# Attention with its inputs prepared one slot ahead, fewer transfers for K and Q, and weight quarters issued by SyncE

## The reference

```
x   = x + tanh(g_xattn) * xattn(layernorm(x), ctx)     # x, ctx: (8, 256, 512) float32
x   = x + tanh(g_ffn)   * moe(layernorm(x))

xattn:  q = Wq x + bq;  k = Wk c + bk;  v = Wv c + bv   # 256 channels, 16 heads of 16
        p = softmax(q k^T / 4) over 512 positions;  out = Wo (p v) + bo
moe:    logits = tokens @ gate_w.T;  top 2 of 12 experts, weights normalized
        out  += (silu(t w1^T) * (t w3^T)) w2^T * weight  # 2048 tokens of 512, hidden 320
```

## Time and profile before

| | us |
|---|---|
| runs | 804.32, 808.91, 809.18 |
| median | 808.91 |
| profiled execution | 802.83 |
| its span | 801.1 |

### The profile page before, as it was taken

One profiled execution on the slowest core, in us unless ns is written; L12 is line 12 of the kernel. 1 busy time (PEld: TensorE's weight loads), 2 busy tenths in 40 slices (PEclk: granted clock), 3 DMA queues, 4 the chain that ended last, 5 costly groups with the idle time before them and its releaser, 6 DMA issues.

```text
span 801.1 us, 14200 instructions
## 1 busy us (share of the span) xinstructions
PE 621.2 (78%) x4169; PEld 270.8 (34%) x4170; DVE 420.0 (52%) x769; ACT 332.0 (41%) x394; POOL 243.0 (30%) x186
## 2 busy tenths in 40 slices
PE   3418849889698897988976523179999999999993
PEld 1101202213122131322311101156666666666661
DVE  4787546667466574657646652944333333333330
ACT  5216637567565666665684200002222222222221
POOL 5203105133141332314202111324444333544322
PEclk9959969999999999999997755569999999999997
DMA  5686886967949688695894747527587776764533
GB/s 159 172 221 179 209 248 172 217 205 194 274 134 249 184 179 256 151 275 165 181 283 150 209 152 262 211 79 208 121 234 201 225 205 185 196 114 83 91 40 41
DMA packets 75374, 146.54 MB, mean 183 GB/s; under 512 B 10757, under 2 KB 36870, under 8 KB 73798
## 3 DMA queue, kind: packets, MB, share of 16 engines
q1 hardware_dynamic: 43664, 68.18, 31.4%
q10 hardware_dynamic: 22038, 55.35, 22.7%
q0 software_dynamic: 9632, 22.55, 14.9%
HBM read 87.85 MB, written 53.74 MB: 177 GB/s over the span
## 4 chain that ended last, share of the span: by engine, by line
PE 43%; DMA 19%; issue 16%; DVE 8%; POOL 5%; SPq 5%; ACT 1%; POOLq 0%; DVEq 0%; ACTq 0%
PE S L1334 15%; PE O L1355 9%; DMA K<-k_parts 8%; PE O L1198 5%; PE MA L1234 4%; DMA out<-yo,slot_out 4%; SPq L480 3%; PE S L1159 3%; DMA zl<-osum 2%; PE S L1321 2%; PE MC L1234 2%; DMA q_parts<-qs 2%; ACT prob L694 1%; PE S L1345 1%; POOL qs L552 1%
## 5 line engine op out<-in xcount | busy, mean ns | idle before, releaser
L694 ACT ACTIVATE prob<-S 128x1024 f32<-128x1024 f32 x256 | 245.8, 1024 | 179.8 <-PE S L1159 146.7
L1334 PE MATMUL S<-W,xT 128*128 x1032 | 149.4, 302 | 1.2 <-DVE xT L1107 1.2
L1198 PE MATMUL O<-prob,V 128*32 128x512 f32 x1024 | 148.1, 642 | 0.0
L1159 PE MATMUL S<-Q,K 49*128 49x512 f16 x512 | 91.4, 406 | 65.4 <-DMA K<-k_parts 42.2
L1334 PEld LDWEIGHTS S<-W,xT 128*128 128x128 f16 x1032 | 99.9, 99 | 38.7 <-issue 1.5
L620 POOL DMA_INDIRECT out<-yo,slot_out x43 | 68.5, 1593 | 116.9 <-DMA out<-yo,slot_out 60.0
L1355 PE MATMUL O<-W,hT 128*128 (+1 forms) x344 | 90.3, 381 | 0.9 <-DVE hT L1127 0.9
L1159 PEld LDWEIGHTS S<-Q,K 49*128 49x128 f16 x512 | 20.2, 94 | 193.6 <-ACT prob L694 135.4
L1115 DVE SCALAR_TENSOR_TENSOR hh<-S,act 128x320 f32<-128x320 f32 x43 | 21.1, 492 | 122.6 <-PE S L1334 122.6
L798 DVE SCALAR_TENSOR_TENSOR wp<-wf,wp 128x1024 f16<-128x1024 f32 x48 | 69.6, 1451 | 1.7
L552 POOL TENSOR_TENSOR cs<-ctx,cs 128x1024 f16<-128x1024 f32 x8 | 17.0, 2125 | 150.1 <-DVE cs L859 150.1
(11 more groups left out here) (153 smaller groups left out, 650.4 us busy)
## 6 DMA issues: line engine op xcount, KB each, us to landing
wf<-wall ACTq DMA_DIRECT2D x48, 512.0 KB, 7.1
weight_parts<-wp ACTq DMA_DIRECT2D x48, 512.0 KB, 4.7
W<-weight_parts SPq DMA_DIRECT2D x10, 2048.0 KB, 9.2
Q<-q_parts SPq DMA_DIRECT2D x48, 128.0 KB, 7.8
K<-k_parts SPq DMA_DIRECT2D x48, 128.0 KB, 8.2
ctx<-ctx_in SPq DMA_DIRECT2D x8, 512.0 KB, 12.5
residual<-x SPq DMA_DIRECT2D x8, 512.0 KB, 13.9
k_parts<-ks SPq DMA_DIRECT2D x8, 512.0 KB, 2.8
```

What stands on the lines that cost most here:

```text
L694: act.activation(prob[:, u % RING, :], S[u % 2][:, :], ACT.Exp, scale=SCALE).then_inc(g.exp, 1)
L1159: last = pe.matmul(S[u % 2][:, s * T:(s + 1) * T], K[par][r0:r0 + PARTS * DK + 1, 2 * g4 + n, st * P:(st + 1) * P], Q[par][r0:r0 + PARTS * ...
L1198: last = pe.matmul(O[g4 % 2][2 * DK * j:2 * DK * (j + 1), :], V[par][:, st, GH * g4 + j, :], prob[:, u % RING, (j % 2) * T:(j % 2 + 1) * T ...
L1334: last = pe.matmul(ps, xT[par][:, xp * TT + k, :], W[:, bass.ds(off + (w * WCOL + (2 * k + n) * F), F)], start=(k == 0 and (xp, w) == (0, 0)),
```

## The change

**Ahead.** The context and x of batch t+1 are loaded at the start of slot t, and cast and normed in it (`x_spread` at step 6, `x_normed` at 8, `ctx_high` at 11). `EXTRA` then starts with `k0` at step 0. V goes in four pieces, and `o1` over two steps.

**K and Q.** The layout in DRAM has a place for each of the three passes. Each high part is written twice and each low part once, in six writes of 256 KB with runs of 2 KB, as soon as the part is there, and four reads of 48 partitions bring them back. Row 48 is used only in the guarded run, so its fills go. Channels lie in another order among the rows, and Wo's rows are loaded to match, in eight transfers.

**Gate.** `lg` takes the turned tokens as weights and streams the 12 gate columns, so `lt` is gone.

**Quarters.** SyncE issues stores and loads. Slot 0 has none, 1 has 4, 2 to 7 have 6 each, 8 has 8.

```diff
-q_dram = nc.dram_tensor("q_parts", [2, C, T], F16).ap()
-k_dram = nc.dram_tensor("k_parts", [2, C, T], F16).ap()
+q_dram = nc.dram_tensor("q_parts", [P // DK, PARTS, DK, CT * T], F16).ap()
+k_dram = nc.dram_tensor("k_parts", [P // DK, PARTS, DK, CT * T], F16).ap()
...
-EXTRA = {3: "k0", 4: "k1", 5: "q0", 7: "q1", 8: "o0", 9: "v0", 10: "o1", 11: "v1", 12: "t0", 13: "t1",
-    14: "lg", 15: "lt"}
-ON_AT, XN2_AT, SPLIT_AT = 6, 11, 6
+EXTRA = {0: "k0", 1: "k1", 2: "q0", 3: "q1", 4: "v0", 5: "v1", 6: "v2", 7: "o0", 8: "o1a", 9: "o1b",
+    10: "v3", 12: "t0", 13: "t1", 14: "lg"}
+ON_AT, LN_AT, XN_AT, XN2_AT, CS_AT, SPLIT_AT = 5, 6, 8, 10, 11, 3
...
+  if t.i is None and t.add in (0, B + 1):
+    return []
+  if t.i is None and t.add == 1:
+    steps, parts = (4, 7, 11, 13), [(At(None, 0, 0), c) for c in range(4)]
...
+    steps = (0, 2, 4, 6, 8, 10, 12, 13)
+    parts = [(At(None, 0, e), c) for e in (NE - 2, NE - 1) for c in range(4)]
...
+    steps = (2, 4, 7, 11, 12, 13)
+    if t.i is None:
+      e = [At(None, 0, 3 * ((t.add - 2) // 2) + n) for n in (1, 2, 3)]
+    else:
+      e = [At(t.i, 3, n) for n in (1, 2, 3)]
+    if t.add % 2 == 0:
+      parts = [(e[0], c) for c in range(4)] + [(e[1], c) for c in range(2)]
+    else:
+      parts = [(e[1], c) for c in range(2, 4)] + [(e[2], c) for c in range(4)]
...
-    slot(eng, At(i, 2, 2), 0, True, True, True)
-    slot(eng, At(i, 2, 3), 1, True, True, True)
-  slot(eng, At(None, 0, B), 0, False, True, True)
-  slot(eng, At(None, 0, B + 1), 1, False, False, True)
+  slot(eng, At(None, 0, 0), 0, True, False, False, True)
+  slot(eng, At(None, 0, 1), 1, True, True, False, True)
+  with eng.Fori(0, (B - 4) // 2) as i:
+    slot(eng, At(i, 2, 2), 0, True, True, True, True)
+    slot(eng, At(i, 2, 3), 1, True, True, True, True)
+  slot(eng, At(None, 0, B - 2), 0, True, True, True, True)
+  slot(eng, At(None, 0, B - 1), 1, True, True, True, False)
+  slot(eng, At(None, 0, B), 0, False, True, True, False)
+  slot(eng, At(None, 0, B + 1), 1, False, False, True, False)
...
+  def store_quarter(e, c):
+    wait(sp, s_wlo, e, 4, c + 1, s_bog)
+    sp.dma_start(w_dram[bass.ds(e.value(), 1), :, :, c * WQ:(c + 1) * WQ]
+           .rearrange("e p h n -> p (e h) n"), wp[c % 2][:, :, :]).then_inc(s_wst[c % 2], 16)
+    e, c = (e, c + 2) if c < 2 else (e.before(-1), c - 2)
+    if e.i is not None or e.add < NE:
+      load_quarter(e, c)
...
-        wait(sp, g.xc, t, 32, 0, s_bog)
-        wait(sp, g.a_free, t, NA, -NA)
-        load_batch(t, par)
+      if p:
+        nxt = t.before(-1)
+        wait(sp, g.cc, nxt, 16, 0, s_bog)
+        wait(sp, g.xc, nxt, 16, 0, s_bog)
+        wait(sp, g.cl, nxt, 1, -1)
+        load_ctx(nxt, 1 - par)
+        load_x(nxt)
+      if not guard and t.i is None and t.add == 1:
+        for n in range(2):
+          load_quarter(At(None, 0, 0), n)
...
-        wait(sp, g.qk, t, 16 * 4 * PARTS, 0, s_bog)
-        wait(sp, g.kl, t, 1, 1)
-        sp.dma_start(k_dram.rearrange("h (m p) t -> p h m t", p=P), ks[:, :, :, :]).then_inc(g.qkst, 16)
-        wait(sp, g.ql, t, 1, 1)
-        sp.dma_start(q_dram.rearrange("h (m p) t -> p h m t", p=P), qs[:, :, :, :]).then_inc(g.qkst, 16)
-        wait(sp, g.qkst, t, 32, 32, s_bog)
+        wait(sp, g.qk, t, KQ_READS, 0, s_bog)
+        for stack, parts, dram, hi, lo, order in ((K, ks, k_dram, g.kh, g.kl, (0, 0, 1)),
+                             (Q, qs, q_dram, g.qh, g.ql, (0, 1, 0))):
+          wait(sp, hi, t, 1, 1)
+          for r in sorted(range(PARTS), key=lambda r: order[r]):
+            if order[r] == 1:
+              wait(sp, lo, t, 1, 1)
+            sp.dma_start(dram[:, r], parts[:, order[r]].rearrange("p m t -> p (m t)"))\
+              .then_inc(g.qkst, 16)
+          if stack is K:
+            weights(0, 3)
+        wait(sp, g.qkst, t, KQ_WRITES, KQ_WRITES, s_bog)
         wait(sp, g.full, t, 2 * VS, -2 * VS)
-        sp.wait_ge(s_rows[par], 4)
-        for s in range(2):
-          for r, (qp, kp) in enumerate(((0, 0), (1, 0), (0, 1))):
-            for stack, dram, part in ((Q, q_dram, qp), (K, k_dram, kp)):
-              src = dram[part].rearrange("(g s c) t -> s c g t", s=2, c=DK)[s]
-              sp.dma_start(stack[par][64 * s + DK * r:64 * s + DK * (r + 1), :, :], src)\
-                .then_inc(g.qk, 16)
+        for stack, dram in ((K, k_dram), (Q, q_dram)):
+          for s in range(2):
+            sp.dma_start(stack[par][64 * s:64 * s + PARTS * DK, :, :]
+                  .rearrange("p (g m) t -> p g (m t)", m=CT),
+                  dram.rearrange("(g s) r c n -> s (r c) g n", s=2)[s]).then_inc(g.qk, 16)
+        weights(3, 8)
+      else:
+        weights(0, 9)
...
+      weights(8 if a else 9, VS)
+    if guard:
+      sp.wait_ge(s_rows, 4)
+    load_ctx(At(None, 0, 0), 0)
+    if not guard:
+      sp.dma_start(w4[:, 0, :, :], WkT.rearrange("(k p) n -> p k n", p=P)).then_inc(s_const, 16)
+    load_x(At(None, 0, 0))
...
-      if c:
-        lo_part(t.before(2), os_, on, g.oh, g.ol)
-      if a:
         lo_part(t, qs, qf, g.qh, g.ql)
       if c:
-        bc = t.before(2)
-        wait(pool, g.mv2, bc, CT, CT, s_pool_c)
-        pool.tensor_scalar(veps2[:, :], mv2[:, :, 1], EPS, None, ALU.add).then_inc(g.veps2, 1)
-        wait(pool, g.veps2, bc, 1, 1)
-        pool.tensor_tensor(rstd2[:, :], veps2[:, :], neg_half[:, :], ALU.pow).then_inc(g.rstd2, 1)
+        lo_part(bc, os_, on, g.oh, g.ol)
+      if p:
+        inverse_spread(nxt, mv, veps, rstd, g.mv, g.veps, g.rstd)
+        lo_part(nxt, xs, xn, g.xh, g.xl)
+      if c:
+        inverse_spread(bc, mv2, veps2, rstd2, g.mv2, g.veps2, g.rstd2)
         wait(pool, g.x2h, bc, 1, 1)
         pool.tensor_tensor(xs2[:, 1], xn2[:, :, :], xs2[:, 0], ALU.subtract).then_inc(g.x2l, 1)
+      if p:
+        lo_part(nxt, cs, ctx_sb[1 - par], g.ch, g.cl)
...
-    if not guard:
-      act.wait_ge(g.xc, 32)
-      for n in range(2):
-        load_quarter(At(None, 0, 0), n)
-      shift_rows(K, SHIFT)
-      shift_rows(Q, 0.0)
...
-        for v, e, c in splits:
-          if u == 2 * min(v + 2, VS - 1) + 1:
-            store_quarter(e, c)
...
+    def ctx_high(b, par):
+      wait(dve, g.cc, b, 16, 16, s_tanh)
+      wait(dve, g.a_full, b, NA)
+      dve.tensor_copy(cs[:, 0], ctx_sb[par][:, :, :]).then_inc(g.ch, 1)
+    def x_spread(b):
+      wait(dve, g.xc, b, 16, 16, s_tanh)
+      for m in range(CT):
+        dve.bn_stats(stats[:, m, :], rest(b, m)).then_inc(g.bst, 1)
+      for m in range(CT):
+        wait(dve, g.bst, b, CT, m + 1, s_tanh)
+        dve.bn_aggr(mv[:, m, :], stats[:, m, :]).then_inc(g.mv, 1)
+    def x_normed(b):
+      wait(dve, g.rstd, b, 1, 1)
+      wait(dve, g.xl, b, 1)
+      for m in range(CT):
+        dve.tensor_scalar(xn[:, m, :], rest(b, m), mv[:, m, 0:1], rstd[:, m:m + 1],
+                 ALU.subtract, ALU.mult).then_inc(g.xn, 1)
+      wait(dve, g.xn, b, CT, CT)
+      wait(dve, g.a_full, b, NA, A_USES["q1"] + 1 - NA)
+      dve.tensor_copy(xs[:, 0], xn[:, :, :]).then_inc(g.xh, 1)
...
+        if c and a and v == 1:
+          inverse_sums(bc, a or b_)
+        if c and v == ON_AT:
...
+        if p and v == LN_AT:
+          x_spread(nxt)
+        if p and v == XN_AT:
+          x_normed(nxt)
...
+        if p and v == CS_AT:
+          ctx_high(nxt, 1 - par)
...
+    def inverse_sums(b, more):
+      wait(dve, g.zl, b, 16, 16)
+      dve.reciprocal(zr[:, :], zl[:, :]).then_inc(g.rz, 1)
+      if not guard:
+        for n, (bound, op) in enumerate(((Z_LEAST, ALU.is_ge), (Z_MOST, ALU.is_le))):
+          wait(dve, g.ok, b, 2, 1 + n)
+          dve.scalar_tensor_tensor(out=ok[:, :], in0=zl[:, :], scalar=bound,
+                      in1=ok[:, :], op0=op, op1=ALU.mult).then_inc(g.ok, 1)
+      if more:
+        return
...
-        for k in range(TT):
-          last = pe.matmul(MC[0:NE, 0:C], gate[:, k, :], xT2[:, :, k * P:(k + 1) * P],
-                  start=(k == 0), stop=(k == TT - 1))
-      last.then_inc(g.c_full, 1)
-    def slot(pe, t, par, a, b_, c):
+          for k in range(TT):
+            last = pe.matmul(MC[:, m * NE:(m + 1) * NE], xT2[:, m, k * P:(k + 1) * P], gate[:, k, :],
+                    start=(k == 0), stop=(k == TT - 1))
+      if n1 == 3 * CT:
+        last.then_inc(g.c_full, 1)
```

340 lines of the change are left out of this document (152 added, 188 removed).

## The result

The change made the kernel slower: 840.83 us in the median of four runs (838.03 to 845.12), against 809.04 for the kernel before on the same chip. The ratio is 1.042, with a 95% interval of 1.036 to 1.048. The forecast was 761. The profiled execution of the changed kernel took 845.12 us, with a span of 843.4.

What follows compares the result with a forecast made beforehand. It took no engine as full: middle slots repeated in 48 to 49 us because context and x were fetched late through one queue. Savings of 15 + 16 + 8 + 0 + 4 = 43 us gave 760, plus 1: 761 us, range 730 to 788.

Steps and rivals of the forecast that it cites:

- Part 1: Slot 0: earlier K and Q reads, taking 7 us, put first scores at 40: 15 us less (8 to 18).
- Part 2: Slot 1: its end waits for no read, 39.5 us for 55.6: 16 us less (12 to 18).
- Part 3: Slots 2 to 7: TensorE's 38.4 plus waits of 5 and 3.5 make 47 a slot: 8 us less.
- (a): Step 1 of slots 2 to 7: VectorE waits for the sums' read behind 2 MB in SyncE's queue, 5 us.
- (b): Steps 11 to 13 of slots 2 to 7: VectorE waits for late weight quarters on two buffers, 3.5 us.
- Part 4: Slot 8: eight quarters, four rounds of splits and loads come to 46 plus the end: 0 (-8 to +4).
- Part 5: Slot 9 and after: splits gone from step 7, cheaper gate, earlier expert loads: 4 us less (1 to 7).
- Rival 1: Middle slots reach TensorE's pace, 42 us each: 38 us less instead of 8, 731; chance 0.2.
- Rival 2: K and Q writes of 8 blocks get half the DMA engines, 4.4 us more: slots of 51, 786; chance 0.2.
- Rival 3: SyncE's queue becomes the clock, quarters 11 and 13 land 6.7 us late in slots 2 to 8: 808 to 855; chance 0.05.

Runs made afterwards that it cites:

- e4: Changed kernel with the K and Q scratch copy laid out so each write is 128 rows (wide writes): 814.91 us, ratio 1.015.
- e6: e4 with no weight quarter in the attention, neither splits nor transfers: mean slot 41.1 us, only slots count.
- e10: e4 with the six splits a slot kept but none of the quarters' transfers: mean slot 50.1 us, only slots count.
- e13: e10 with the splits at steps 1, 3, 6, 8, 13, 14: mean slot 47.3 us, only slots count.
- e16: e14 with the quarters issued by SyncE instead of GpSimd: 859.39 us, ratio 1.070.
- e14: e8 with the quarters issued by GpSimd and the splits at steps 1, 3, 6, 8, 13, 14: 781.30 us, ratio 0.973.
- e17: Changed kernel with only the quarters issued by GpSimd and the splits at steps 1, 3, 6, 8, 13, 14: 783.64 us, ratio 0.973.
- e7: e4 with the quarters issued by GpSimd, in the order of the splits: 798.89 us, ratio 0.989.
- e8: e4 with context and x loaded behind the sums' transfers (sums first), quarters still by SyncE: 805.38 us, ratio 1.001.
- e18: e14 with splits at 2, 4, 6, 9, 13, 14, two of slot 8's quarters in slot 9, each expert's weights waited for separately: 771.12 us, ratio 0.954.

## Why the prediction was wrong

By stage, against the forecast's own time of 760 for the profiled execution:

**Part 1, slot 0: partly right.** 9 us less, not 15. The last read went out at 35.2 and took 10.77 us, which lies inside my bounds of 4.3 to 14; I had taken 7. One premise was false, that nothing else is under way: right behind the reads, from 35.8 to 37.7, SyncE issues the next context and x and two quarters, 2 MB, and the engines are full until 46 (share 1.03, at 185 GB/s). The later issue is the narrow write (reads 2.3 us earlier in e4).

**Part 2, slot 1: nearly right.** 42.0 us for 39.5; the saving was 13.6.

**Part 3, slots 2 to 7: wrong by 82 of the 85 us.** I had 38.4 for TensorE and 8.5 for the two waits. TensorE's pace is 41.1 (e6), 2.7 more; 1 of it is the gate (below). Two steps failed.

**The first is the price of (a) and (b), 5 and 3.5.** I named both places and priced them as waits of VectorE. In slot 3 of the changed kernel VectorE waits 8.74 us for the sums and TensorE stands 6.70 behind that; VectorE waits 5.14 for the quarter of step 11 and TensorE stands 6.54. Behind the two it works at its low level, 2.4 and 1.5 us more. That makes 17 us for my 8.5, and with the pace 58 of the slot's 60.9. The sum had nothing for the clock. It had the late load at 7.1 us from issue to landing; the chain has 11.64, from an issue at 190.03 that SyncE's list held back behind a write of Q (8.01) and four reads.

**The second is the sentence "VectorE's own work rises from 30.7 by two quarters of about 2.2 to 35, still under the slot"**, which priced the splits at nothing by a sum over the slot. The rows that mattered were local: at steps 10 to 13 VectorE casts the normed tokens and the context, drains a bank of sums, takes three splits and must copy the turned tokens in time for TensorE. With no transfer of weights at all the splits cost 9.0 us a slot (e10 against e6). In the slot shown, 10.4 over e6, the wait for that copy (4.45) and the low clock behind it (5) make up nearly all. With the splits moved (e13) 6.2 of the 9.0 stay; splits stretch in other places there. I did put (b) at this place, but as a stall of VectorE, and did not ask who is queued behind it there.

The slots of e6, e10, e4 and the changed kernel (41.1, 50.1, 55.6, 59.8) give 9.0 for the splits, 5.5 for their transfers and 4.2 for the narrow writes. These are steps of one ladder and not shares of the loss. In the changed kernel the split of step 11 is not stretched (0.69 and 1.23 at 201.75); it comes late instead. And the order in which terms are taken out changes their sizes: taken out first, the narrow writes give 26 us; taken out last, with sums first, nothing clear of noise.

**Part 4, slot 8: right by its number**, 48.4 us for 49; no run tests its rounds of splits and loads. **Part 5 and after: 8 us less for my 4**, though the gate with tokens as weights costs 1.96 us at the high clock and 3.59 at the low one, not the 1 that I took and over my bound of 1.8; the old one took the same 3.59 at the low clock.

**Rival 1** (TensorE's pace) is what the new pipeline makes without the weights: 41 us a slot. **Rival 2** (half the engines) was true, with its price: 4.4 us a slot forecast, 4.2 measured. I gave it 0.2 and stopped there. **Rival 3** (SyncE's queue as the clock) named the place and the result, 808 to 855. The waits before the splits of steps 11 and 13 are 5.14 and 4.68 us in slot 3, each under its 6.7 and together 9.8, above the 6 a slot from which it was to decide; over the kernel they are 77.5. e16 against e14 shows the queue, e17 against the changed kernel shows it with the position. I gave it 0.05 because I took the cases as exclusive. They stacked, and the range left that out.

What stays open: how the 57 us of e17 divide between position and issuing engine in the changed kernel itself; each alone was run only with wide writes, where the engine by itself gave 16 us (e7 against e4; 2.7% by the ratios) and the steps by themselves made it slower in SyncE's list (e16 against e8) and faster in GpSimd's (e14 against e7, with sums first as well). What the clock's fall costs behind a wait (5 us in the slot of e10, 1.5 and 2.4 in the changed kernel) is read from rows, not tried. That VectorE stands, rather than works slowly, beside GpSimd is read from rows as well, and e18 takes out only the second halves.

## What to carry to other kernels

An engine's sum of work against the length of a slot tells nothing about an instruction put ahead of one that the bounding engine waits for: look at the two or three steps in which it will stand, at what is queued behind it, and at what GpSimd does there. A wait of VectorE is priced by how long TensorE stands behind it. A transfer that waits belongs in the list of an engine that has nothing else to wait for. And where several rivals lengthen the same path, price them together as well as apart.

## What the runs showed of the hardware

- VectorE's split beside GpSimd's subtraction takes 3.04 us instead of 1.23 (second half, e17) and 1.33 to 2.56 instead of 0.69 (first half, e18).
- Writes of 256 KB in 8 blocks of 16 rows of 2 KB move at 193 GB/s with a DMA share of 0.51, in 128 rows at 369 GB/s with 0.96, with nothing else under way.
- GpSimd issues a 512 KB transfer in 0.56 to 1.14 us (median 0.7), beside a busy VectorE, and the fastest versions have it do so. The same page of the Trainium skill (SBUF — State Buffer, SBUF: two separate sides) warns that VectorE can starve such transfers and advises another queue; here the other queue, SyncE's, was 78 us slower for its waits (859.39 against 781.30).
- After a wait of 4.45 us TensorE ran at its low level for about 10 us (e10), after one of 6.54 us for 3.3 (changed kernel).
